# Delta rule stage of a 15-stage decoder: the formings of a unit move behind the groups of products, the projections between the couplings

## The chip, the cores and the metric

The kernel runs on one core of one Trainium2 chip. The metric is the device time of one execution in microseconds (us); lower is better. Three runs of the kernel before gave a median of 6915.6 us (6914.33 to 6922.18).

The engines are named as the profile names them: PE (TensorE, matrix multiplies into PSUM), DVE (VectorE), ACT (ScalarE), POOL (GpSimd). Each takes its instructions strictly in the program's order; they meet at semaphores.

## The reference

The whole reference is a decoder of four layers (attention, cross attention and feed forward in each), run over x of 16 sequences x 128 positions x 256 features. The change lies in its first step alone, a gated delta rule with 8 heads of size 64 and M = 8 modes. Cut to what matters:

```python
q = (x @ Wq).reshape(B, T, H, DK)
k = (x @ Wk).reshape(B, T, H, DK)
v = (x @ Wv).reshape(B, T, H, DV)
beta = sigmoid(x @ Wbeta); tg = sigmoid(x @ Wtg)          # one per head and mode
qr = l2norm(rotary(q, cos, sin)) * scale; kr = l2norm(rotary(k, cos, sin))
g = log(clip(tg * rho, 1e-06))
def step(S, inp):                                         # scanned over the T positions
    q_t, k_t, v_t, b_g, b_beta = inp
    S = S * exp(b_g)[..., None, None]
    kv = einsum('mbhk,mbhkv->mbhv', k_t, S)
    dv = (v_t[None] - kv) * b_beta[..., None]
    S = S + k_t[..., :, None] * dv[..., None, :]
    return S, einsum('mbhk,mbhkv->mbhv', q_t, S)
o = einsum('tmbhv,hm->bthv', ys, softmax(mode_logits))
x = layernorm(x + (o * sigmoid(x @ Wg)) @ Wo)
```

The kernel doesn't scan. For each of the head-mode pairs the recurrence over 128 positions is a triangular system, which is solved in blocks of 32 positions: the four 32x32 diagonal blocks are inverted, and the solution is built up quarter by quarter.

## The kernel before

`delta_stage` is the first of 15 stages. Its loop runs over the B = 16 sequences, one **turn** each (turn 0 and turn 15 are written out, 1 to 14 are a loop), and a turn has two **halves** of 4 heads. A half of a sequence is a **unit**: unit u = 2g is the first half of sequence g, u + 1 the second. A unit has 32 head-mode pairs, taken in GROUPS = 8 groups of four. The order on every engine is written out by hand, in a function `turn` for each engine (PE L886, ACT L1056, DVE L1300, POOL L698).

What a unit goes through, with the functions and lines:

- `phase` (PE L816), for each group i: three matmul steps put the decay exponents of four pairs into bank 0 (L824 to L828), ACT takes them through Exp (`decays`, L1017), four key and query products go to banks 4 and 5 (i even) or 1 and 2 (i odd) (L843), and DVE multiplies products and decays into NB (`take_products`, L1182). Exponents i + 1 wait for decays i, products i + 2 for the taking of products i. The rotated keys and queries that the products read are made by DVE (`rotate`, L1166) and POOL (`add_halves`, L691, two additions for each pair of groups, started when both of DVE's halves are there).
- `take_lower` (ACT L1024) copies the diagonal blocks out when the products are taken; `invert` (DVE L1203) inverts them in a chain of 61 small linked steps (L1219, L1224, L1225, L1227). Steps of the next sequence's projections (sums of squares L1241, decays, normalising L1248, splitting of the logarithms L1271 to L1279, and two parts of rounding L1283, L1289) are placed at given positions of that chain in the first half, two rotations at positions 40 and 46 in the second. DVE works in order: a placed step that has to wait holds up the inversion behind it.
- `spread` (ACT L1040) puts the inverse into the block diagonal Df; `form` (PE L798) multiplies Df with group i of the unit (8 matmul instructions of 128x256), and `take_formed` (ACT L1006) copies it back into NB (L1011, L1013). `set_identities` (ACT L1032) writes the diagonal blocks.
- `couple(u, half, q)` (PE L848), q = 1, 2, 3: for each of 4 heads one carrier matmul (L734) and 8 couplings, 16 matmul instructions of 64 columns (L860); `solutions` (ACT L1049) takes each head. `output` (PE L865) and `project_out` (L880) follow, and DVE adds and normalises.
- For the next sequence: `turn_x` (PE L736), `project_qk` (L743), `project_bt` (L751), `sum_logs` (L758), `turn_qk` (L769), `swap` (L777), `project_v` (L783), with `take_x`, `square` (L967), `sigmoids`, `logarithms`, `take`, `take_v` on ACT. `project_gates` (L790) and `take_gates` (L1000) serve the sequence at hand.

The order around the change, as PE has it in a turn. **First half**: the 8 groups of `phase` for unit u + 1, with forming 0 of unit u behind group 2 and forming 1 behind group 5, the earlier sequence's `project_out` behind group 4; then gates, form 2, turn_x, form 3, project_qk, form 4, project_bt, form 5 to 7, couple 1, sum_logs, turn_qk, couple 2, swap, couple 3, output. **Second half**: the 8 groups of `phase` for unit u + 2 (the next sequence), again with two formings (of unit u + 1) inside, then form 2 to 4, project_v, form 5 to 7, couple 1 to 3, output. ACT follows the same order. The formings use banks 6 and 7, and those of groups 3, 5 and 7 banks 4 and 5, so that one can run while ACT empties the other.

## Time and profile before

| | us |
|---|---|
| median of 3 runs | 6915.6 |
| the profiled execution | 6926.1 |
| its span on the core | 6924.3 |
| delta rule stage, in the span | about 95 to 2520 |
| one turn in the middle (first half, second half) | 74.86 + 75.46 = 150.3 |
| PE busy in this turn | 64.73 + 61.35 = 126.1 |
| DVE busy in this turn | 51.47 + 46.20 = 97.7 |

A span's views are in us from its start. In a timeline a line is one instruction or a run of like ones; the bracket is the idle time of the engine before it and what ended it. "issue" there means that the profile names no releaser.
### The profile page before, as it was taken

To read this page: it belongs to the slowest core of one execution; us is meant where nothing else is said; L and a number is where in the kernel's file an instruction comes from. 1 tells how busy PE (TensorE), PEld (TensorE's weight loads), DVE (VectorE), ACT (ScalarE), POOL (GpSimd) and SP (SyncE) were. 2 spreads that over 40 slices of the span, in tenths; PEclk is the share of its full clock that TensorE was granted. 3 is DMA by queue.
4 is the path that set the end of the run, shared out by engine and by line. 5 is a ranking of instruction groups with operands and counts; after the bars stand their busy time and mean duration, and the time that the engine had idled before them with its cause. 6 is when DMAs were issued, how large, how long until landed. Compare 5 with 4: busy or idle time off the path is not lost. (4 is left out here: it accounts for less than half of the span.)

```text
span 6924.3 us, 79364 instructions
## 1 busy us (share of the span) xinstructions
PE 5430.9 (78%) x28132; PEld 3808.8 (55%) x28132; DVE 3468.1 (50%) x7576; ACT 2177.9 (31%) x3691; POOL 1032.2 (15%) x845
## 2 busy tenths in 40 slices
PE   3888888888888875999998877547678467788698
PEld 1666666666666654566665555324356235565454
DVE  6666666666666633000004545558825445544445
ACT  2554544555454431212121222311123322232111
POOL 1212222222212212000002222000001002222000
PEclk8888888888888887999998878755578578888799
DMA  0000000000000000000000000000000000000000
GB/s 31 1 1 1 1 1 1 1 1 1 1 1 1 1 20 39 13 12 24 12 12 7 0 26 9 11 3 0 0 34 0 5 8 0 21 6 1 12 18 24
DMA packets 13489, 63.01 MB, mean 9 GB/s; under 512 B 1168, under 2 KB 5648, under 8 KB 11152
## 3 DMA queue, kind: packets, MB, share of 16 engines
q1 hardware_dynamic: 13200, 59.17, 2.4%
q8 instruction: 180, 2.95, 0.2%
q14 instruction: 109, 0.89, 0.0%
HBM read 57.07 MB, written 2.10 MB: 9 GB/s over the span
## 5 line engine op out<-in xcount | busy, mean ns | idle before, releaser
L1484 PE MATMUL psum<-arena 128*128 128x512 f32 x1600 | 706.6, 595 | 58.4 <-DVE Y L1548 35.8
L812 PE MATMUL psum<-arena 128*128 128x256 f32 x2048 | 559.8, 430 | 60.8 <-ACT arena L1013 59.6
L1565 DVE SCALAR_TENSOR_TENSOR Y<-psum,arena,Y 128x256 f32<-128x256 f32 x416 | 172.5, 477 | 847.9 <-PE psum L1496 847.9
L860 PE MATMUL psum<-arena 64*32 64x64 f32 (+2 forms) x6144 | 596.9, 272 | 0.0
L1496 PE MATMUL psum<-arena 128*128 128x256 f32 x2624 | 583.0, 380 | 4.1 <-DVE arena L1589 4.1
L1189 DVE TENSOR_TENSOR arena<-psum,arena 128x1024 f32<-128x1024 f32 x256 | 313.2, 1223 | 511.3 <-PE psum L843 331.4
L696 POOL TENSOR_TENSOR arena<-arena 128x512 f32<-128x512 f32 x256 | 327.1, 1298 | 1580.4 <-DVE arena L1179 1580.4
L1496 PEld LDWEIGHTS psum<-arena 128*128 128x128 f32 x2624 | 499.3, 190 | 111.8 <-issue 43.5
L1484 PEld LDWEIGHTS psum<-arena 128*128 128x128 f32 x1600 | 304.4, 191 | 409.1 <-issue 341.4
L812 PEld LDWEIGHTS psum<-arena 128*128 128x128 f32 x2048 | 429.4, 216 | 179.1 <-ACT arena L1013 74.5
L860 PEld LDWEIGHTS psum<-arena 64*32 64x32 f32 (+2 forms) x6144 | 517.5, 144 | 13.9 <-issue 7.8
L144 POOL TENSOR_TENSOR arena<-arena,eps 128x4 f32<-128x4 f32 (+2 forms) x76 | 15.0, 197 | 3234.9 <-DVE arena L139 3234.9
L843 PE MATMUL psum<-arena 64*128 64x256 f32 x2048 | 298.7, 411 | 129.2 <-POOL arena L696 129.2
L1530 ACT ACTIVATE arena<-psum,arena 128x512 f32<-128x512 f32 x256 | 175.9, 687 | 701.5 <-PE psum L1484 701.5
L422 PE MATMUL psum<-ident,arena 128*128 128x128 f32 x1280 | 218.0, 326 | 210.0 <-ACT arena L493 210.0
L402 PE MATMUL psum<-arena 128*128 128x512 f32 x640 | 356.8, 691 | 16.8 <-ACT arena L482 11.2
L1225 DVE TENSOR_TENSOR weights<-weights 128x30 f32<-128x30 f32 (+14 forms) x960 | 335.0, 349 | 33.5
L1224 DVE TENSOR_TENSOR weights<-weights 128x30 f32<-128x30 f32 (+14 forms) x960 | 331.0, 345 | 31.0
L1053 ACT ACTIVATE arena<-psum 32x512 f32<-32x512 f32 x384 | 226.2, 589 | 377.0 <-PE psum L860 376.4
L414 PEld LDWEIGHTS psum<-arena 128*128 128x128 f32 x2048 | 284.8, 217 | 101.6 <-issue 61.5
L422 PEld LDWEIGHTS psum<-ident,arena 128*128 128x128 f32 x1280 | 179.2, 171 | 232.2 <-ACT arena L493 232.0
L300 POOL TENSOR_TENSOR arena<-arena,weights 128x1024 f32<-128x1024 f32 x128 | 242.3, 1901 | 407.4 <-PE psum L402 341.7
(435 smaller groups left out, 8881.8 us busy)
## 6 DMA issues: line engine op xcount, KB each, us to landing
arena<-in_experts_L_ffn SPq DMA_DIRECT2D x8, 2052.0 KB, 8.3
arena<-in_ctxT SPq DMA_DIRECT2D x16, 512.0 KB, 3.3
arena<-in_experts_L_ffn SPq DMA_DIRECT2D x18, 384.0 KB, 3.0
weights<-in_w_L_attn SPq DMA_DIRECT2D x1, 3106.0 KB, 13.3
weights<-in_w_L_ffn SPq DMA_DIRECT2D x1, 3072.0 KB, 10.0
weights<-in_w_L_ffn SPq DMA_DIRECT2D x1, 2753.0 KB, 12.0
weights<-in_w_L_relu SPq DMA_DIRECT2D x1, 2436.0 KB, 8.9
X<-in_x SPq DMA_DIRECT2D x1, 2048.0 KB, 8.3
```

The costliest lines, as they stand in the source:

```text
L402: mm = nc.tensor.matmul(out[:, b * 4:b * 4 + 4, :], qT[:, c, u * P:(u + 1) * P], km[:, at % 2, b * 4:b * 4 + 4, :], start=True, stop=True)
L414: mm = nc.tensor.matmul(o_psum[:, c * HH + h, :], pT[:, j % 2, h, :], v, start=True, stop=True)
L422: mm = nc.tensor.transpose(pt_psum[:, h, :], pr[:, j % 2, h, :], k.ident[:, :])
L696: pool.tensor_tensor(both_, both_, t1[:, j, :, :], ALU.add).then_inc(s["rotated"], 1)
L812: mm = nc.tensor.matmul(ps[:, at + j // 2, (j % 2) * 2 * P:(j % 2 + 1) * 2 * P], Df[:, c, :], both(hf)[:, :, c, :], start=True, stop=True)
L843: mm = nc.tensor.matmul(ps[:, bank, m * 2 * P:(m + 1) * 2 * P], kq[rows, i // 2 % 2, at, 0, :], kq[rows, i // 2 % 2, at, :, :], start=True ...
L860: mm = nc.tensor.matmul(ps[n:n + Q, 4 + h, m * DK:(m + 1) * DK], NB[0:n + Q, 2 * (u_odd), place(h, m), n:n + Q], ur[0:n + Q, h, m, :], sta ...
L1189: dve.tensor_tensor(both(hf)[:, :, group, :].rearrange("p k c t -> p c k t"), products, bc(NB[:, 2 * hf + 1, group, :], 2, 2), ALU.mult).t ...
L1224: linked(dve.tensor_tensor(part, bc(inv[:, j + 1:, j], 2, j), bc(inv[:, j, 0:j], 1, below), ALU.mult))
L1225: linked(dve.tensor_tensor(inv[:, j + 1:, 0:j], inv[:, j + 1:, 0:j], part, ALU.add))
L1484: mm = nc.tensor.matmul(ps[:, bank, :], W[s][name][:, c, f * P:(f + 1) * P], xT[:, g, c, :], start=(c == 0), stop=(c == C - 1))
L1496: mm = nc.tensor.matmul(out, h[:, m % 2, f, u * P:(u + 1) * P], W[s]["w2"][:, f, :], start=(f == 0), stop=(f == FC - 1))
```

## The change

PE and ACT: in both halves forming i - 1 of the one unit now stands behind group i of `phase` of the other, for i = 1 to 7, so seven formings lie inside the phase and one (7) behind it. All but forming 7 use banks 6 and 7, and each of them waits for the one before to be copied; forming 7 uses banks 4 and 5. In the first half `turn_x` stands behind forming 7, then couple 1, `project_qk` and `project_bt`, couple 2, `sum_logs` and `turn_qk`, couple 3, `swap`, output. In the second half `project_v` stands in front of forming 7, and the couplings follow it. ACT takes in the same order; `set_identities` moves behind `logarithms` (first half) and behind the solutions of couple 1 (second half). DVE: five of the placed steps of the first half's inversion move by two positions (squares to 18, splitting to 36 and 38, first part to 50). Nothing is added to or taken from the work.

```diff
--- before.py
+++ after.py
@@ -800,13 +800,11 @@
                 if i == 0:
                     pe.wait_ge(s["inverse_ready"], u + 1)
                     need(pe, "solution_ready", u * (NQ - 1) * HALF)
-                elif i < 4:
+                elif i < 7:
                     pe.wait_ge(s["couplings_formed"], u * GROUPS + i)
-                else:
-                    pe.wait_ge(s["couplings_formed"], u * GROUPS + i - 1)
-                if i == 3 and products is not None:
+                elif products is not None:
                     pe.wait_ge(s["products_taken"], products)
-                at = 4 if i in (3, 5, 7) else 6
+                at = 4 if i == 7 else 6
                 for j in range(4):
                     c = 4 * i + j
                     mm = nc.tensor.matmul(ps[:, at + j // 2, (j % 2) * 2 * P:(j % 2 + 1) * 2 * P], Df[:, c, :],
@@ -887,41 +885,35 @@
                 u = g * HALVES
                 for i in range(GROUPS):
                     phase(g, u + 1, 1, i)
-                    if i in (2, 5):
-                        form(u, 0, i // 3)
+                    if i:
+                        form(u, 0, i - 1)
                     if i == 4 and (not isinstance(g, int) or g):
                         project_out(g - 1)
                 project_gates(g)
-                form(u, 0, 2)
+                form(u, 0, 7, (u + 1) * GROUPS + GROUPS - 1)
                 if more:
                     turn_x(g + 1)
-                form(u, 0, 3, (u + 1) * GROUPS + GROUPS - 1)
+                couple(u, 0, 1)
                 if more:
                     project_qk(g + 1)
-                form(u, 0, 4)
-                if more:
                     project_bt(g + 1)
-                for i in range(5, GROUPS):
-                    form(u, 0, i)
-                couple(u, 0, 1)
+                couple(u, 0, 2)
                 if more:
                     sum_logs(g + 1)
                     turn_qk(g + 1)
-                couple(u, 0, 2)
+                couple(u, 0, 3)
                 if more:
                     swap(g + 1)
-                couple(u, 0, 3)
                 output(u, g, 0, 0)
                 output(u, g, 0, 1)
                 for i in range(GROUPS):
                     if more:
                         phase(g + 1, u + 2, 0, i)
-                    if i in (2, 5):
-                        form(u + 1, 1, i // 3)
-                for i in range(2, GROUPS):
-                    form(u + 1, 1, i, (u + 2) * GROUPS + GROUPS - 1 if more and i == 3 else None)
-                    if more and i == 4:
-                        project_v(g + 1)
+                    if i:
+                        form(u + 1, 1, i - 1)
+                if more:
+                    project_v(g + 1)
+                form(u + 1, 1, 7, (u + 2) * GROUPS + GROUPS - 1 if more else None)
                 couple(u + 1, 1, 1)
                 couple(u + 1, 1, 2)
                 couple(u + 1, 1, 3)
@@ -1006,7 +998,7 @@
             def take_formed(u, hf, i):
 
                 act.wait_ge(s["formed"], u * GROUPS + i + 1)
-                at = 4 if i in (3, 5, 7) else 6
+                at = 4 if i == 7 else 6
                 formed = ps[:, at:at + 2, :].rearrange("p b (c k t) -> p (b c) k t", c=2, k=2)
                 nc.scalar.copy(NB[:, 2 * hf + 1, 4 * i:4 * i + 4, :], formed[:, :, 1, :])
                 for q in range(1, NQ):
@@ -1057,53 +1049,45 @@
                 u = g * HALVES
                 for i in range(GROUPS):
                     decays(u + 1, 1, i)
-                    if i in (2, 5):
-                        take_formed(u, 0, i // 3)
+                    if i:
+                        take_formed(u, 0, i - 1)
                     if i in (5, 6):
                         take_lower(u + 1, 1, 0, (2 * i - 10, 2 * i - 9))
                 take_lower(u + 1, 1, 1, range(NQ))
                 take_gates(g)
-                take_formed(u, 0, 2)
+                take_formed(u, 0, 7)
                 if more:
                     take_x(g + 1)
-                take_formed(u, 0, 3)
+                solutions(u, 1)
                 if more:
                     square(g + 1)
-                take_formed(u, 0, 4)
-                if more:
                     sigmoids(g + 1)
-                for i in range(5, GROUPS):
-                    take_formed(u, 0, i)
-                    if i == 5:
-                        set_identities(u + 1, 1)
+                solutions(u, 2)
                 if more:
                     logarithms(g + 1)
-                solutions(u, 1)
+                set_identities(u + 1, 1)
                 if more:
                     round_sums(g + 1)
                     take(g + 1, qkT, "qk_turned", "qkT_ready")
                     round_rest(g + 1)
-                solutions(u, 2)
+                solutions(u, 3)
                 if more:
                     take(g + 1, qkS, "swapped", "swapped_ready")
-                solutions(u, 3)
                 spread(u + 1)
                 for i in range(GROUPS):
                     if more:
                         decays(u + 2, 0, i)
-                    if i in (2, 5):
-                        take_formed(u + 1, 1, i // 3)
+                    if i:
+                        take_formed(u + 1, 1, i - 1)
                     if more and i in (5, 6):
                         take_lower(u + 2, 0, 0, (2 * i - 10, 2 * i - 9))
                 if more:
                     take_lower(u + 2, 0, 1, range(NQ))
-                for i in range(2, GROUPS):
-                    take_formed(u + 1, 1, i)
-                    if more and i == 4:
-                        take_v(g + 1)
-                    if more and i == 5:
-                        set_identities(u + 2, 0)
+                    take_v(g + 1)
+                take_formed(u + 1, 1, 7)
                 solutions(u + 1, 1)
+                if more:
+                    set_identities(u + 2, 0)
                 solutions(u + 1, 2)
                 solutions(u + 1, 3)
                 if more:
@@ -1312,11 +1296,11 @@
                     state["ch"].end()
                 steps = []
                 if more:
-                    steps += [(16, lambda: sum_squares(g + 1)), (22, lambda: scale_decays(g + 1)),
+                    steps += [(18, lambda: sum_squares(g + 1)), (22, lambda: scale_decays(g + 1)),
                               (24, lambda: clip_decays(g + 1)), (32, lambda: normalise(g + 1)),
-                              (38, remember("views", lambda: split(g + 1))),
-                              (40, lambda: split_rest(g + 1, state["views"])),
-                              (52, lambda: first_part(g + 1)), (58, lambda: second_part(g + 1))]
+                              (36, remember("views", lambda: split(g + 1))),
+                              (38, lambda: split_rest(g + 1, state["views"])),
+                              (50, lambda: first_part(g + 1)), (58, lambda: second_part(g + 1))]
                 if not first:
                     steps += [(2, remember("ch", lambda: finish(g - 1))), (14, applied)]
                 invert(u + 1, between(*steps))
```

## Rows read from the trace of the kernel before

**Rows 1.** The page: span of the profiled execution, and busy time of each engine.

```profile
span 6924.3 us, 79364 instructions
PE 5430.9 (78%) x28132; PEld 3808.8 (55%) x28132; DVE 3468.1 (50%) x7576; ACT 2177.9 (31%) x3691; POOL 1032.2 (15%) x845
```

**Rows 2.** Busy time in stretches: first half, second half of a turn, whole stage.

```profile
core 0: us, PE busy (x) PEld busy (x) DVE busy (x) ACT busy (x) POOL busy (x), PEclk, DMA share, GB/s
1201.93:1276.79 74.86, 64.73 (x507) 50.05 (x507) 51.47 (x107) 39.47 (x80) 18.95 (x17) 0.91 0.01 1
1276.79:1352.25 75.46, 61.35 (x450) 48.08 (x449) 46.20 (x88) 35.53 (x71) 14.06 (x12) 0.80 0.00 1
...
95.00:2520.00 2425.00, 2009.98 (x15220) 1564.82 (x15220) 1553.57 (x3103) 1192.50 (x2386) 522.35 (x462) 0.85 0.01 2
```

**Rows 3.** Timeline of PE, first half: start us, length us, instructions [idle before <-releaser].

```profile
1201.93 0.38 PE L824 MATMUL psum<-arena 128*128 128x512 bf16 x1 [2.73 <-issue]
...
1208.91 1.13 PE L843 MATMUL psum<-arena 64*128 64x256 f32 x8 [2.51 <-POOL arena L696]
1209.97 1.99 PE L812 MATMUL psum<-arena 128*128 128x256 f32 x8
1211.80 0.38 PE L824 MATMUL psum<-arena 128*128 128x512 bf16 x1
...
1232.78 0.41 PE L740 MATMUL psum<-ident,weights 128*128 128x128 f32 x2 [2.16 <-ACT arena L1003]
...
1236.41 4.33 PE L748 MATMUL psum<-weights 128*128 128x512 f32 x8
...
1251.04 0.16 PE L734 MATMUL psum<-arena 128*128 128x1 bf16 x1 [2.95 <-issue]
```

**Rows 4.** Timeline of PE: second half, and the last turn of the stage.

```profile
1307.14 6.58 PE L812 MATMUL psum<-arena 128*128 128x256 f32 x16 [3.12 <-ACT arena L1013]
...
1323.56 0.16 PE L734 MATMUL psum<-arena 128*128 128x1 bf16 x1 [2.94 <-issue]
...
2476.99 1.99 PE L812 MATMUL psum<-arena 128*128 128x256 f32 x8 [1.14 <-ACT arena L1013]
...
2493.35 0.16 PE L734 MATMUL psum<-arena 128*128 128x1 bf16 x1 [1.19 <-issue]
```

**Rows 5.** Timeline of DVE over the same turn.

```profile
1203.86 1.23 DVE L1189 TENSOR_TENSOR arena<-psum,arena 128x1024 f32<-128x1024 f32 x1 [14.35 <-PE psum L843]
...
1230.76 1.91 DVE L1219 STREAM_TRANSPOSE weights<-weights 128x1024 f32<-128x1024 f32 x1 [2.65 <-ACT weights L1029]
...
1241.41 1.22 DVE L1241 TENSOR_REDUCE arena<-arena 128x16 f32<-128x1024 f32 x1 [2.37 <-ACT arena L970]
...
1254.46 0.22 DVE L1279 TENSOR_TENSOR weights<-arena,weights 128x64 f32<-128x64 f32 x1
...
1269.49 0.69 DVE L1174 TENSOR_TENSOR arena<-arena,weights 128x512 f32<-128x512 f32 x1 [1.88 <-ACT arena L984]
...
1280.08 1.23 DVE L1189 TENSOR_TENSOR arena<-psum,arena 128x1024 f32<-128x1024 f32 x1 [4.58 <-ACT arena L1021]
...
1306.04 1.92 DVE L1219 STREAM_TRANSPOSE weights<-weights 128x1024 f32<-128x1024 f32 x1 [2.65 <-ACT weights L1029]
...
1334.07 2.07 DVE L1227 STREAM_TRANSPOSE weights<-weights 128x1024 f32<-128x1024 f32 x1
```

**Rows 6.** Timeline of ACT over the same turn.

```profile
1228.14 2.58 ACT L1029 ACTIVATE weights<-arena 32x512 f32<-32x512 f32 x4 [1.36 <-DVE arena L1189]
...
1278.09 1.28 ACT L1021 ACT_TABLE_LOAD   x1
...
1346.30 4.20 ACT L1046 COPY arena<-weights 32x1024 f32<-32x1024 f32 x4
```

**Rows 7.** Busy time in stretches in which PE runs couplings alone.

```profile
1323.60:1343.60 20.00, 20.00 (x175) 18.13 (x176) 13.18 (x27) 5.66 (x10) 2.60 (x2) 0.50 0.01 2
2493.40:2506.70 13.30, 13.30 (x204) 12.08 (x204) 0.00 (x0) 6.48 (x11) 0.00 (x0) 1.00 0.01 1
```

## The prediction

> **What bounds the kernel now.** I read the page first for the size of the stage, then the stretches of one turn in the middle, then the timelines of PE, DVE and ACT over that turn, to see which wait ends last at each place. The stage takes 2425 us of the span of 6924.3 [rows 1, 2]. A turn takes 74.86 + 75.46 = 150.3 us; PE is busy for 64.73 + 61.35 = 126.1 of it and DVE for 97.7 [rows 2]. So no engine is full, but PE is the nearest to it, and the reader should see two losses of PE.
>
> The first is idle time, 10.1 us in the first half and 14.1 in the second. It has few places: 2.5 us before the third group of products, which waits for POOL's rotation; 2.2 before turn_x, whose bank ACT frees with the gates; 2.95 before the first coupling of either half, where ACT is two copies behind; 3.1 before the forming at 1307.14, which waits for the copy of the last [rows 3, 4]; and 2.7 at the loop's end.
>
> The second loss is the clock. Behind the 2.94 us of idling at 1323.56 PE runs the couplings at a granted clock of 0.50 for 20 us: 175 instructions, at 17 to a head 10.3 heads, so 1.94 us a head. In the last turn the wait at the same place is 1.19 us, the clock stays at 1.00, and 204 instructions (12 heads) take 13.3 us, 1.11 a head [rows 4, 7]. Twelve heads cost 23.3 us or 13.3.
>
> DVE isn't the bound yet: it waits 14.35 us for the first products of the first half, and 4.58 for ACT's decays in the second [rows 5]. It will matter what is left of these 19 us.
>
> **The change, part by part.** Nothing is added; all gains and losses are waits and clock. I walk through one new turn from a = 0, the start of the first taking of products in the first half (1203.86 in the old turn [rows 5]). Three steps repeat: exponents and products of a group, 1.83 us (1209.97 less 1.13 and the exponents before it, and the same as eight groups without waits give); a forming, 1.83 us (1209.97 to 1211.80) [rows 3]; a forming with the copy behind it on ACT, 3.13 us (1.99 and the 1.14 waited [rows 4]).
>
> *First half, phase.* A group and a forming together are 3.66 us. The rotation chain runs from the taking of products 0 (1203.86) to products 2 (1208.91), 5.05 us [rows 3, 5]. PE now has one more forming in it, so the wait of 2.5 falls to 0.7, and the later ones vanish (a pair of groups now takes 7.3 us). The copy of a forming has 3.66 us before the next one needs the bank and takes 3.13, so the single pair of banks costs nothing; if the copy took over 0.5 us longer, every step would. The last group ends at 26.2, forming 6 at 28.0, gates at 29.9, forming 7 at 31.7. ACT copies forming 6 until 29.3 and only then takes the lower blocks (2.58 us [rows 6]): DVE's inversion starts at 31.9. It started at 1230.76 - 1203.86 = 26.9 [rows 5], so it loses 5.0.
>
> *Between phase and couplings.* ACT then loads its table and takes the gates (1.9 us), and turn_x starts at 33.9 after 2.1 us of idling, as before (2.16). The copy of forming 7 ends at 34.8, and couple 1 starts at 34.9 instead of 1251.04 - 1203.86 = 47.2 [rows 3, 5]. But project_qk (4.3 us [rows 3]) and project_bt (half as many matmuls of a quarter of the columns, 0.5) have gone behind it.
>
> *Couple 1 and the squares.* In the old turn idling of 2.2 and 0.4 us at this place was followed by a lower clock at project_qk (eight matmuls in 4.33 us; at the high clock some 3.5). Now 2.1 and 0.5 stand right before couplings, which haven't brought the clock back by themselves for 20 us [rows 7]. If it falls: couple 1 7.4 us, project_qk 5.6 (its first half still low). If not: 4.5 and 3.5. Bounds for the pair are 8.0 and 14.8 (all low). The sum of squares on DVE starts 0.7 behind project_qk (1236.41 + 4.33 to 1241.41 [rows 3, 5]): at 48.7, or 43.7. DVE's chain arrives there at 41.0 (31.9, and 9.1 us for the 18 links; 16 took 8.3), so it waits **7.7 or 2.7 us** where it waited 2.37. This is the new wait of the change; behind it stands the whole inversion.
>
> *The logarithms.* From the start of the sum of squares to the end of splitting were 1254.46 + 0.22 - 1241.41 = 13.2 us with 24 links between [rows 5]; now 20 links, 1.7 less: 11.5. sum_logs on PE can start at 60.2, or 55.2. PE is ready (bt 0.6, couple 2 4.5) at 53 or 48, so it idles for **7 us**, and the clock falls; sum_logs and turn_qk take some 4.5, couple 3 4.5 to 5, swap 1.8 (as many columns as a forming), ACT's copy 0.7. The swapped keys are there at 72.0 or 67.0. DVE has ended its inversion by then (70 or 65), so its rotation follows at once. From there to the first taking of the second half it is two rotations (four steps of 0.6, 2.4), POOL's pair (2.6, which is the 5.05 from above less a taking and half a rotation) and the products (1.1), with half a microsecond for DVE and POOL in each other's way 6.6 us; ACT's spread and table load (4.20 + 1.28 + 0.6 [rows 6]) fit under it. So the second half's first taking is at **78.6 or 73.6**, against 1280.08 - 1203.86 = 76.2: the first half loses 2.4 or gains 2.6.
>
> *Second half*, from b = 0 at that taking. The same walk without project_out: inversion starts at 30.0 (before: 1306.04 - 1280.08 = 26.0 [rows 5]). project_v and forming 7 are done at 29.8, couple 1 starts at 31.6 after 1.8 us of idling, nearer to the 1.19 that left the clock up than to 2.94. Couplings end at 45, or 55 if it falls; with output 3.7 (what the 26 us from the first coupling to the loop's end leave beside 12 heads) and the loop's 2.7, PE is back at 51 or 61. DVE inverts in 1334.07 + 2.07 - 1306.04 = 30.1 us [rows 5], so the inverse is there at 60.1; ACT spreads it by 64.3 (4.20 [rows 6]), and the next decays follow, 64.9, first taking 65.0. **DVE and ACT are the bound here**, at either clock of PE. The one cost that I can't see is ACT's own turn of the loop, which was hidden. DVE's is below 1.0 and PE's 2.7 [rows 3]; 0 and 2.7 are the ends, and I take 1.0, since ACT's instructions are few and long like DVE's. So 66.0, against 150.3 - 76.2 = 74.1: a gain of 8.1.
>
> *set_identities*, 3.15 us on ACT, now stands between solutions of couplings 1 and 2 in the second half; PE has 4.5 us of couple 2 above it, and it is free. If it weren't, it would cost up to 3 us of PE that isn't the bound. In the first half it stands under the 7 us of idling.
>
> **The sum.** A new turn takes 78.6 + 66.0 = 144.6 us when the clock falls before couple 1, and 139.6 when it doesn't. The same idling fell on a lower clock in each old turn, but it is now split by turn_x a little differently; I take two turns in three low: 143.0, a gain of 7.3. Fifteen turns give 110. The last turn gains about 7 in its first half and loses 4 in its second, where seven formings stand alone at 3.13 us with one pair of banks. The first turns have less to gain; I take 10 off. Against the profiled execution of 6926.1 that is 6823; that execution is 10 us over the median of the runs, so the forecast is **6815 us**.
>
> A rule of the Trainium skill stands against one step. Rows 7 show couplings alone for 20 us at 0.50 with PE busy throughout. "TensorE: Matmul & The Clock Gate", section "Part 1: The HAM clock gate", has it that sustained activity releases the throttle. By that rule couple 1 would win its clock back before it ends; the trace disagrees. It is the first rival below.
>
> **Rivals.**
> 1. *The clock stays up or comes back during couple 1.* Then every turn takes 139.6: 15 x 10.7 less the 10, about 6765. For it: 1.19 us of idling was harmless, and PE's other waits shrink. Against: rows 7, and 2.6 us idle of 3.2 just before. Chance 0.13.
> 2. *ACT pays PE's price at the loop and the clock is low in each turn*: 146.3, gain 4.0, 15 x 4.0 less the 7 is 6863. Chance 0.09.
> 3. *Slower: the low clock holds through the whole first half.* Couple 1 at 7.8 leads into project_qk all low (7.0), couple 2 doesn't raise it, and after 7 us of idling sum_logs, turn_qk, couple 3 (7.8) and swap (3.5) are low as well. Squares at 50.5, split at 62, swapped keys at 79, taking at 85.6: the first half loses 9.4 and the second gains 8.1 less what ACT's loop costs beyond 1.0. That is +1.3 to +3.0 a turn, 6935 to 6960. It decides when low stretches add up to over 30 us of the half; the old half had 10 around couple 1, and full-width matmuls ended them. Chance 0.12.
> 4. *No change*: each step of the phase is 0.5 us longer than its matmuls, because ACT now has decays and copy in each (1.7 of 3.66 us, and 1.3 more of lower blocks in two of them). That is 7 us over both phases, the whole gain; 6915. ACT has the room by the rows, so 0.06.
>
> **How the numbers follow.** The forecast has 0.60: 6815, with its own range 6790 to 6840. The range wanted holds rivals 1 and 2 and most of the forecast's errors: 6755 to 6880; outside remain rivals 3 and 4 (0.18). Faster by over 0.2% (14 us, about what a measurement of this kernel can tell): 0.60 + 0.13 + 0.09 = 0.82; same 0.06; slower 0.12.
>
> **What would show it.** In the changed turn: forming and group in steps of 3.66 with one wait of about 0.7; couple 1 35 us behind the first taking; a wait of DVE before L1241 of 3 to 8 us; PE idle for some 7 before L763; second half 66 us from first taking to first taking, with PE waiting for ACT's decays (L1021) right after the loop. The forecast is wrong if PE's couplings of the second half still end last, if L763 doesn't wait, or if steps in the phase are longer than 3.66.

## The result: faster by 0.6%, a third of what was forecast

Over eleven executions of each, the changed kernel has a median of 6882.1 us (6837.0 to 6888.1) and the kernel before 6914.3 us (6904.4 to 6922.2). The ratio is 0.9942, with a 95% interval of 0.9924 to 0.9961. The forecast was 6815, with a range of 6755 to 6880. The direction was right; the gain is 32 us where 100 were forecast, and the time lies just above the range.

| | before | forecast | changed |
|---|---|---|---|
| median, us | 6914.3 | 6815 | 6882.1 |
| profiled execution, us | 6926.1 | | 6883.7 |
| a turn in the middle | 150.3 | 143.0 (139.6 or 144.6) | 146.75 |
| first half, taking to taking | 76.2 | 73.6 or 78.6 | 81.24 |
| second half, taking to taking | 74.1 | 66.0 | 65.51 |

The changed kernel's executions fall in two groups, two of the eleven at 6837 to 6838 with a mean granted clock of 0.825 and nine at 6880 to 6888 with 0.815 or 0.816; in a run shown further down a turn of the shorter kind is profiled.

These are the stretches of the changed kernel's turn, cut at the first taking of products of each half (columns as in [rows 2]):

```profile
span 6881.9 us, 79230 instructions
...
1180.11:1261.35 81.24, 68.91 (x504) 52.24 (x508) 50.32 (x108) 41.77 (x82) 18.99 (x17) 0.84 0.00 1
1261.35:1326.86 65.51, 56.79 (x446) 44.79 (x449) 45.89 (x89) 32.52 (x68) 14.11 (x12) 0.81 0.01 2
```

PE is still busy for 126 us of the turn, but the granted clock, PEclk, is lower than before in the first half (0.84, it was 0.91 [rows 2]). The second half has become 8.6 us shorter, the first 5.0 us longer. The timeline of DVE shows where (it answers to [rows 5]; L1203 is the start of an inversion, L1225 the sum of squares, L1173 the taking of products):

```profile
1213.63 1.92 DVE L1203 STREAM_TRANSPOSE weights<-weights 128x1024 f32<-128x1024 f32 x1 [3.03 <-ACT weights L1021]
...
1231.33 1.22 DVE L1225 TENSOR_REDUCE arena<-arena 128x16 f32<-128x1024 f32 x1 [8.62 <-ACT arena L962]
...
1254.18 0.69 DVE L1158 TENSOR_TENSOR arena<-arena,weights 128x512 f32<-128x512 f32 x1 [0.59 <-ACT arena L976]
...
1261.35 1.23 DVE L1173 TENSOR_TENSOR arena<-psum,arena 128x1024 f32<-128x1024 f32 x1 [1.18 <-PE psum L841]
...
1291.81 1.92 DVE L1203 STREAM_TRANSPOSE weights<-weights 128x1024 f32<-128x1024 f32 x1 [3.03 <-ACT weights L1021]
...
1326.86 1.23 DVE L1173 TENSOR_TENSOR arena<-psum,arena 128x1024 f32<-128x1024 f32 x1 [2.71 <-ACT arena L1013]
```

The new wait is the 8.62 us before L1225: DVE stands in the middle of the inversion and waits for the squares, which wait for project_qk, which now stands behind couple 1. The old one was 2.37. On PE the same turn reads (answers to [rows 3, 4]):

```profile
1215.66 0.41 PE L740 MATMUL psum<-ident,weights 128*128 128x128 f32 x2 [2.24 <-ACT arena L995]
1216.55 0.16 PE L734 MATMUL psum<-arena 128*128 128x1 bf16 x1 [0.48 <-issue]
...
1224.36 6.29 PE L748 MATMUL psum<-weights 128*128 128x512 f32 x8
...
1243.00 0.80 PE L763 MATMUL psum<-weights 128*128 128x128 f32 x2 [7.53 <-DVE weights L1263]
...
1293.43 0.16 PE L734 MATMUL psum<-arena 128*128 128x1 bf16 x1 [1.91 <-issue]
...
1320.83 0.38 PE L823 MATMUL psum<-arena,weights 128*128 128x512 bf16 x1 [2.98 <-issue]
...
1326.81 0.61 PE L822 MATMUL psum<-arena 128*128 128x512 bf16 x1 [3.73 <-ACT arena L1013]
```

Waits of 2.24 and 0.48 us stand before couple 1, 7.53 before sum_logs, 1.91 before couple 1 of the second half, and at the turn's end 2.98 and 3.73. Couple 1 and the greater part of project_qk run at the low clock, and so do heads two to ten of the second half's couplings and the start of the next phase:

```profile
1216.60:1230.50 13.90, 13.90 (x77) 9.58 (x78) 5.47 (x20) 3.06 (x6) 0.75 (x2) 0.53 0.00 1
1294.60:1310.30 15.70, 15.70 (x138) 14.22 (x137) 14.43 (x40) 7.72 (x11) 0.00 (x0) 0.50 0.01 2
1326.80:1332.00 5.20, 5.19 (x18) 3.34 (x19) 4.10 (x6) 0.60 (x1) 2.49 (x2) 0.50 0.00 0
```

### The profile page after: what moved, and what is told of

It reads as the page before. It is cut to its first block and busy times, and to the rows that moved or that the text cites. A ratio compares the mean times of both kernels' runs of the same rounds, so it can differ in the third digit from the quotient of the medians.

```text
span 6881.9 us, 79230 instructions
## 1 busy us (share of the span) xinstructions
PE 5420.1 (79%) x28029; PEld 3790.1 (55%) x28132; DVE 3447.2 (50%) x7576; ACT 2165.4 (31%) x3691; POOL 1033.8 (15%) x845
## 5 line engine op out<-in xcount | busy, mean ns | idle before, releaser
L1480 PE MATMUL psum<-arena 128*128 128x256 f32 x2624 | 583.0, 380 | 4.1 <-DVE arena L1573 4.1
L1480 PEld LDWEIGHTS psum<-arena 128*128 128x128 f32 x2624 | 499.3, 190 | 111.7 <-issue 43.5
L1173 DVE TENSOR_TENSOR arena<-psum,arena 128x1024 f32<-128x1024 f32 x256 | 313.5, 1224 | 458.7 <-ACT arena L1013 237.6
L1468 PEld LDWEIGHTS psum<-arena 128*128 128x128 f32 x1600 | 304.4, 191 | 409.1 <-issue 341.4
L810 PE MATMUL psum<-arena 128*128 128x256 f32 x2048 | 520.4, 398 | 9.8 <-ACT arena L1005 6.9
L810 PEld LDWEIGHTS psum<-arena 128*128 128x128 f32 x2048 | 379.3, 195 | 139.9 <-issue 84.2
L841 PE MATMUL psum<-arena 64*128 64x256 f32 x2048 | 329.3, 445 | 57.9 <-POOL arena L696 57.9
L1209 DVE TENSOR_TENSOR weights<-weights 128x30 f32<-128x30 f32 (+14 forms) x960 | 335.0, 349 | 33.5
L414 PEld LDWEIGHTS psum<-arena 128*128 128x128 f32 x2048 | 284.8, 217 | 101.7 <-issue 61.6
```

The source lines that it names most:

```text
L414: mm = nc.tensor.matmul(o_psum[:, c * HH + h, :], pT[:, j % 2, h, :], v, start=True, stop=True)
L810: mm = nc.tensor.matmul(ps[:, at + j // 2, (j % 2) * 2 * P:(j % 2 + 1) * 2 * P], Df[:, c, :], both(hf)[:, :, c, :], start=True, stop=True)
L841: mm = nc.tensor.matmul(ps[:, bank, m * 2 * P:(m + 1) * 2 * P], kq[rows, i // 2 % 2, at, 0, :], kq[rows, i // 2 % 2, at, :, :], start=True ...
L1173: dve.tensor_tensor(both(hf)[:, :, group, :].rearrange("p k c t -> p c k t"), products, bc(NB[:, 2 * hf + 1, group, :], 2, 2), ALU.mult).t ...
L1209: linked(dve.tensor_tensor(inv[:, j + 1:, 0:j], inv[:, j + 1:, 0:j], part, ALU.add))
L1468: mm = nc.tensor.matmul(ps[:, bank, :], W[s][name][:, c, f * P:(f + 1) * P], xT[:, g, c, :], start=(c == 0), stop=(c == C - 1))
```

## The experiments

The theory after the result: the changed kernel's **first half is bound by a chain through the next sequence's projections** (couple 1, project_qk, squares, splitting, sum_logs, couple 3, swap), its length set partly by PE's clock in couple 1 and project_qk; the **second half by DVE's inversion and ACT's spread**. I shall call it theory A. The rivals: the new order of projections helps and the loss is elsewhere; DVE's inversion is the bound everywhere and its wait was free; PE's low clock in the second half is what a turn pays. In each group of runs the kernel before ran on the same chip: 6919.2 for the first four, 6916.4 for the next four, 6905.0 for the last two. Differences in us to the changed kernel take its median of 6882; an execution of its shorter group (6837) is 45 us below that.

### The two parts apart

**Only the moved formings** (the changed kernel with the old order behind the first half's phase; PE's part, ACT's order and DVE's positions follow it):

```diff
                 if more:
                     turn_x(g + 1)
-                couple(u, 0, 1)
-                if more:
                     project_qk(g + 1)
                     project_bt(g + 1)
-                couple(u, 0, 2)
+                couple(u, 0, 1)
                 if more:
                     sum_logs(g + 1)
                     turn_qk(g + 1)
-                couple(u, 0, 3)
+                couple(u, 0, 2)
                 if more:
                     swap(g + 1)
+                couple(u, 0, 3)
```

> The changed kernel with the first half's old order behind the phase: project_qk and project_bt ahead of couple 1, sum_logs and turn_qk behind couple 1, swap behind couple 2, DVE's steps at their old positions; only the moved formings of the change are left. Theory A (the first half of the changed kernel is bound by the chain couple 1, project_qk, squares, splitting of the logarithms, sum_logs, and couple 1 standing ahead of project_qk lengthens it): DVE waits under 1 us before L1225 instead of 8.6, a turn is 138 to 141 us instead of 146.8, time about 6760 to 6800. Rival B (the projections between the couplings help, as they fill PE's waits): slower than the changed kernel, over 6882. Rival C (a turn is bound by DVE's inversions wherever PE's steps stand): no change, 6875 to 6890.

Measured: 6831.9 us, ratio 0.9872 (0.9855 to 0.9888); a turn is 143.4 us. Rival B falls, and rival C by its range; but the changed kernel's own shorter group, which the sections below come to, is as fast as this run (6837, 143.4 a turn). DVE's wait before the squares is 0.7 us, as theory A had it, but the turn missed A's 138 to 141 and the time its 6760 to 6800 by 32 us. The reason is on PE:

```profile
1160.80:1239.06 78.26, 64.51 (x504) 49.27 (x508) 50.39 (x107) 41.77 (x82) 18.94 (x17) 0.88 0.00 1
1239.06:1304.19 65.13, 55.17 (x446) 43.93 (x450) 46.50 (x89) 32.52 (x68) 14.12 (x12) 0.86 0.01 2
...
1216.99 0.80 PE L763 MATMUL psum<-weights 128*128 128x128 f32 x2 [9.19 <-DVE weights L1261]
```

In the old order sum_logs stands behind couple 1 alone, and with the formings gone from this place nothing is left in front of it: PE waits 9.19 us for the splitting, and then has couples 2 and 3 still to do before output. So the change's order has a good step (sum_logs behind couple 2) and a bad one (project_qk behind couple 1). The run with project_qk first, further down, has the good step without the bad one and is 74 us faster than this.

**Only the couplings' new order**, with the formings where they were (PE's part again):

```diff
                 form(u, 0, 3, (u + 1) * GROUPS + GROUPS - 1)
-                if more:
-                    project_qk(g + 1)
-                form(u, 0, 4)
-                if more:
-                    project_bt(g + 1)
-                for i in range(5, GROUPS):
+                for i in range(4, GROUPS):
                     form(u, 0, i)
                 couple(u, 0, 1)
                 if more:
+                    project_qk(g + 1)
+                    project_bt(g + 1)
+                couple(u, 0, 2)
+                if more:
                     sum_logs(g + 1)
                     turn_qk(g + 1)
-                couple(u, 0, 2)
+                couple(u, 0, 3)
                 if more:
                     swap(g + 1)
-                couple(u, 0, 3)
```

> The kernel before with the other part of the change alone: the formings stay where they were (two inside the phase, six behind it), but couple 1 stands ahead of project_qk and project_bt, couple 2 ahead of sum_logs, couple 3 ahead of swap, DVE's steps at their new positions. Theory A: the squares come some 8 us later than in the kernel before, sum_logs waits for the splitting, a turn gets 5 to 10 us longer than before, time 6985 to 7060. Rival B (this part helps by itself): under 6905.

Measured: 6983.6 us, ratio 1.0092 (1.0075 to 1.0108), 1 us under theory A's 6985 to 7060; its 5 to 10 us a turn are 4.1 on average over the loop (153.9 where the kernel before has 149.8). Rival B falls. By itself this part makes the kernel slower. DVE waits in the inversion for

```profile
1290.46 1.22 DVE L1235 TENSOR_REDUCE arena<-arena 128x16 f32<-128x1024 f32 x1 [19.07 <-ACT arena L968]
```

19 us, and the first half takes 86.0 us in this turn, where it took 76.2. In most other turns of this run the wait is 17.5 us and the half 83.5.

### One step undone, one wait filled

**project_qk ahead of couple 1**, all else as changed:

```diff
                 if more:
                     turn_x(g + 1)
-                couple(u, 0, 1)
-                if more:
                     project_qk(g + 1)
                     project_bt(g + 1)
+                couple(u, 0, 1)
                 couple(u, 0, 2)
```

with `square` and `sigmoids` ahead of the first solutions on ACT, `logarithms` ahead of the second. This brings back the old place of the step, and with it what the clock does there.

> The changed kernel with one thing undone: project_qk and project_bt stand ahead of couple 1 again (with their ACT steps ahead of the solutions, and logarithms ahead of the second solutions). Everything else as changed. Theory A: DVE's wait before L1225 falls from 8.6 to under 1 us, the wait of PE before L763 from 7.5 to under 4, the second half starts 6 to 9 us earlier in the turn, which is 138 to 141 us; time 6755 to 6800. Rival C (DVE's inversion is the bound in the first half too, and its wait was free): 6875 to 6890. Rival D (only the clock before couple 1 counts): couple 1 at the high clock, and no more than 4 us a turn, 6820 to 6850.

Measured: 6757.8 us, ratio 0.9764 (0.9748 to 0.9781), in theory A's range; C and D fall. The placing of this one step, its clock included, costs 6882 - 6758 = 124 us (79 against the shorter group), more than the 87 us (6919 - 6832) that the moved formings gain in the old order. The lines that answer to those above:

```profile
1124.19:1196.16 71.97, 62.37 (x504) 48.10 (x508) 50.30 (x107) 41.86 (x82) 19.02 (x17) 0.93 0.00 1
1196.16:1262.09 65.93, 56.63 (x446) 44.70 (x449) 45.60 (x89) 32.52 (x68) 14.11 (x12) 0.84 0.01 2
...
1166.03 1.21 DVE L1224 TENSOR_REDUCE arena<-arena 128x16 f32<-128x1024 f32 x1
...
1177.71 0.79 PE L763 MATMUL psum<-weights 128*128 128x128 f32 x2 [4.57 <-DVE weights L1262]
```

DVE no longer waits for the squares, PE waits 4.57 instead of 7.53 us before sum_logs (a little over the "under 4" expected), the first half is 9.3 us shorter and the second is the same but for 0.4. The turns of the loop alternate between 137.9 and 138.6 us. Couple 1 runs at the high clock here (1.08 us for a head's 16 couplings, 1.91 in the changed kernel); what the clock alone is worth is for the next run to tell.

**Idle matmuls before couple 1 of the first half**, to keep the clock up:

```diff
+            def warm(n, taken=None):
+                if taken is not None:
+                    pe.wait_ge(s["products_taken"], taken)
+                for _ in range(n):
+                    nc.tensor.matmul(ps[:, 1, 0:D], ident_h, later_h[:, 0:2, :], start=True, stop=True)
...
                 form(u, 0, 7, (u + 1) * GROUPS + GROUPS - 1)
+                warm(18, (u + 2) * GROUPS)
                 if more:
                     turn_x(g + 1)
+                warm(5)
                 couple(u, 0, 1)
```

> The changed kernel with idle matmuls (18 bf16 ones of 256 columns into the free bank 1 before turn_x, 5 behind it) where PE waits 2.2 and 0.5 us ahead of couple 1 in the first half. No work is left out. Theory A with the clock as the forecast had it: the clock stays at 1.00 through couple 1 and project_qk, which take 4.5 and 3.5 us instead of 7.8 and 6.1, the squares come some 5 us earlier, and a turn is 140 to 142 us instead of 146.8; 6790 to 6820. Rival C (DVE-bound): no change. Rival E (couplings by themselves bring the clock down, filled wait or not): granted clock 0.50 in couple 1 as before, no change.

Measured: 6806.8 us, ratio 0.9837 (0.9821 to 0.9854), in theory A's range. Couple 1 runs at the full clock and the wait before the squares falls to 2.60:

```profile
1139.44:1215.36 75.92, 66.02 (x527) 51.35 (x531) 50.44 (x107) 41.97 (x82) 19.00 (x17) 0.90 0.00 1
1215.36:1280.48 65.12, 54.25 (x446) 42.82 (x449) 46.48 (x88) 32.52 (x68) 14.12 (x12) 0.85 0.01 2
1175.80:1180.40 4.60, 4.60 (x70) 4.17 (x70) 4.14 (x16) 1.97 (x5) 0.75 (x2) 1.00 0.00 0
...
1184.61 1.22 DVE L1234 TENSOR_REDUCE arena<-arena 128x16 f32<-128x1024 f32 x1 [2.60 <-ACT arena L971]
```

The wait before sum_logs is 7.53 us as before, and the turns are 140.2 to 141.1 us. So the low clock in couple 1 and project_qk costs 75 us of the 124 in this place, and the order by itself the other 49. Against the shorter group the same two runs give 30 and 49. That the clock only costs because project_qk stands behind couple 1 is argued from the chain; no run has the low clock in couple 1 with project_qk ahead of it.

### The second half

**Idle matmuls before couple 1 of the second half alone** (`warm(18, (u + 3) * GROUPS)` ahead of `couple(u + 1, 1, 1)`):

> The changed kernel with 18 idle matmuls into bank 1 ahead of couple 1 in the second half alone, where PE waits 1.9 us and then runs ten heads of couplings at the low clock. No work is left out. Theory A (the second half is bound by DVE's inversion and ACT's spread, 65.1 to 65.9 us in every kernel so far, with the couplings done 9 to 14 us before): couplings at the high clock, PE ready some 8 us earlier, and no gain: a turn 146 to 147 us, time 6870 to 6890. Rival F (PE's low clock there is what a turn pays): 8 us a turn, about 6765.

Measured: 6837.0 us, ratio 0.9886 (0.9869 to 0.9902). Neither expectation on the time held. On the mechanism theory A did:

```profile
1160.84:1239.14 78.30, 66.22 (x507) 50.69 (x508) 50.40 (x108) 41.98 (x82) 19.02 (x17) 0.87 0.00 1
1239.14:1304.21 65.07, 51.73 (x467) 39.79 (x466) 46.43 (x89) 32.32 (x68) 14.10 (x12) 0.90 0.01 2
1271.00:1284.30 13.30, 13.30 (x205) 12.00 (x205) 12.02 (x37) 9.29 (x14) 0.00 (x0) 1.00 0.02 3
```

The couplings of the second half now run at 1.00 and end 45.2 us behind the first taking instead of 52.9, and the half is 65.07 instead of 65.51: 7.7 us of PE's time gave 0.4 at most. Rival F falls. But the first half, which was not touched, is 78.30 instead of 81.24. Couple 1 there loses the clock later than it did and takes 6.1 us instead of 7.8, and the squares come 3.5 us earlier. This first half is the one of the changed kernel's own shorter group, shown in the next run (78.24), and so is the time (6837). The filler didn't make a new pattern; all four executions with it are of the shorter one, where 7 of 23 without it are (two of eleven, and three and two of six in the next two runs). That suggests that what PE does in one half bears on where the low stretches fall in the other.

**Ten tiny memsets in the second half's inversion**, meant as a delay of 1 us:

```diff
-                    invert(u + 2, between((40, lambda: rotate(g + 1, u + 3, 1, 0, 0)),
+                    idle = [(at, lambda n=at - 22: dve.memset(logs[:, 12 * n:12 * n + 12], 0.0)) for at in range(22, 32)]
+                    invert(u + 2, between(*idle, (40, lambda: rotate(g + 1, u + 3, 1, 0, 0)),
```

> The changed kernel with ten tiny memsets (12 columns each) placed between links of the second half's inversion, about 1 us of DVE in all. If a turn is a plain chain through that inversion: the second half 66 to 66.8 us, a turn 147.5 to 148, 8 to 15 us slower, 6890 to 6900. If the turn's length is held by where its low stretches of PE's clock fall (as the second group of executions and the fillers in the second half suggest): a turn unchanged to 0.1 us, or 3 us off to either side, with the first half making up the difference: 6880 to 6885 or about 6837 or 6930.

As a delay it failed: each memset takes 0.07 us between two links and the inversion lasts 30.1 us as before. It is in effect the changed kernel again (median 6859.0, ratio 0.994, 0.9911 to 0.997), and its six executions show both groups: three at 6831 to 6837, three at 6881. The profiled one is of the shorter group:

```profile
1163.70:1241.94 78.24, 66.17 (x507) 50.59 (x508) 50.33 (x108) 41.97 (x82) 19.01 (x17) 0.87 0.00 1
1241.94:1307.07 65.13, 54.33 (x449) 42.63 (x448) 46.62 (x99) 32.52 (x68) 14.10 (x12) 0.85 0.01 2
...
1211.34 1.22 DVE L1225 TENSOR_REDUCE arena<-arena 128x16 f32<-128x1024 f32 x1 [5.73 <-ACT arena L962]
```

A turn is 143.37 us; DVE's wait before the squares is 5.73 instead of 8.62, and the second half is 65.13 instead of 65.51. **The changed kernel once more:**

> The changed kernel itself once more, for its profile: 6880 to 6884 with turns of 146.8 us, or (two of eleven executions so far) 6837 with turns that I expect at 143.4 us, in which the first half has a shorter low stretch around couple 1 and the second half is the same 65.1 to 65.5.

Measured: median 6880.3; four executions at 6880 to 6885, two at 6830 and 6837; ratio 0.9941 (0.9914 to 0.9968). Its profile is of the longer group and repeats the first one: 81.27 and 65.47 us. So the two groups differ by 3.4 us a turn, 3.0 of it in the first half, where the squares come 3.6 us earlier. In either group every turn of the middle repeats the last one to 0.1 us, low stretches included. What sends an execution into the one or the other stays open. The same turn of 143.37 us, to 0.02 us, stands in three kernels whose waits differ: in this one, in the one with the moved formings alone and in the one with the second half's wait filled. So a turn isn't the plain sum of its steps, and differences of up to 3.4 us a turn (some 50 us) between two of these kernels may come from the pattern and not from the edit. What sets it stays open too.

### What is left, and a better balance

**project_qk early and fillers in three places** (18 before turn_x, 18 before couple 1 of the second half, and 16 behind the first group of products of the first half):

> The kernel with project_qk and project_bt ahead of couple 1 (run before at 6758), with idle matmuls before turn_x (18), before couple 1 of the second half (18) and behind the first group of products of the first half (16). Theory A (both halves are now bound by DVE's inversions and what hangs on them, PE's clock hardly counts): 0 to 2 us a turn, 6725 to 6758. Rival F (PE's clock is the bound): over 4 us a turn, under 6700.

Measured: 6754.4 us, ratio 0.9767 (0.9750 to 0.9783), as theory A had it: 3 us less than the 6757.8 without the fillers on another chip, and by the ratios (0.9767 and 0.9764) nothing. With project_qk early, filling the waits before the couplings is worth nothing.

**The same fillers in the changed kernel** (and 5 behind turn_x):

> The changed kernel with idle matmuls in all three places (18 and 5 around turn_x, 18 before couple 1 of the second half, 16 behind the first group of products of the first half). Theory A (beyond couple 1, the clock low at the start of the phase costs the first half what the forecast missed): the inversion of the first half starts 31.9 to 32.3 us behind the first taking instead of 33.5, a turn is 138.5 to 140.5 us against about 141 with the first two fillers alone, 6770 to 6800. If the low clock at the phase's start costs nothing: equal to the run with the fillers around turn_x alone, 6800 to 6812.

Measured: 6802.4 us, ratio 0.9835 (0.9818 to 0.9851), 4 us under the run with the first two fillers, and by the ratios (0.9835 and 0.9837) equal to it. From the second turn on the turns are 140.2 to 141.2 us, as there, not 138.5 to 140.5. The inversion starts between 32.8 and 34.0 us behind the first taking, without the steady gain expected. The third filler didn't do what it was meant for, and PE's timeline shows why (L741 is the filler):

```profile
1274.34 3.60 PE L741 MATMUL psum<-arena 128*128 128x256 bf16 x16
1282.49 0.61 PE L829 MATMUL psum<-arena 128*128 128x512 bf16 x1 [4.56 <-ACT arena L1026]
...
1282.50:1287.50 5.00, 5.00 (x18) 3.16 (x19) 3.92 (x6) 0.60 (x1) 2.46 (x2) 0.50 0.02 3
```

Its products had been taken long before, so it runs at once and 4.56 us of idling are left behind it; the next 5 us of the phase are at 0.50 as they were. It is the same in the run before (4.57). So neither run says what the low clock at the phase's start costs. By the profile alone, the first group's products and the first forming take 2.08 and 2.86 us in the changed kernel, where later ones take 1.13 and 1.99: 1.8 us together.

**Three formings inside the phase instead of seven**, on top of project_qk early:

```diff
                     phase(g, u + 1, 1, i)
-                    if i:
-                        form(u, 0, i - 1)
+                    if i in (1, 3, 5):
+                        form(u, 0, i // 2)
...
                 project_gates(g)
-                form(u, 0, 7, (u + 1) * GROUPS + GROUPS - 1)
+                form(u, 0, 3, (u + 1) * GROUPS + GROUPS - 1)
+                form(u, 0, 4)
                 if more:
                     turn_x(g + 1)
+                form(u, 0, 5)
+                if more:
                     project_qk(g + 1)
+                form(u, 0, 6)
+                if more:
                     project_bt(g + 1)
+                form(u, 0, 7)
```

with the banks in turn as in the kernel before, and the same in the second half. Three things change at once against the run with project_qk first: the number of formings in the phase, the banks, and the projections between the formings.

> The same order with project_qk early, but only three formings inside each phase (behind groups 1, 3 and 5) and five behind it, with the two pairs of banks in turn as in the kernel before, project_v between formings 4 and 5 in the second half. Theory A (a forming inside the phase puts off the products and so the inversion of the other unit by 1.83 us, and the inversions are now the bound): inversions start 26 to 28 us behind the first taking instead of 33 and 25 to 26 instead of 30; the second half takes 60 to 61 us from taking to taking instead of 65.1; a turn 128 to 134 us, time 6600 to 6700. Rival G (the formings back behind the phase bring back the idling and the low clock of the kernel before, PE becomes the bound): a turn 139 us or more, 6760 to 6850.

Measured: **6663.4 us**, ratio 0.9631 (0.9613 to 0.9649): faster than both kernels, by 253 and by about 220 us; rival G's times fall. Timeline of DVE (L1218 starts an inversion, L1226 ends it), and the stretches:

```profile
1113.94 1.96 DVE L1218 STREAM_TRANSPOSE weights<-weights 128x1024 f32<-128x1024 f32 x1 [2.65 <-ACT weights L1029]
...
1122.99 1.21 DVE L1240 TENSOR_REDUCE arena<-arena 128x16 f32<-128x1024 f32 x1
...
1180.01 1.98 DVE L1218 STREAM_TRANSPOSE weights<-weights 128x1024 f32<-128x1024 f32 x1 [2.65 <-ACT weights L1029]
...
1086.59:1154.48 67.89, 60.15 (x507) 45.53 (x507) 52.43 (x107) 41.47 (x82) 19.46 (x17) 0.98 0.00 1
1154.48:1217.22 62.74, 56.12 (x449) 43.59 (x449) 47.49 (x88) 32.64 (x68) 14.54 (x12) 0.85 0.01 2
...
992.42 0.16 PE L734 MATMUL psum<-arena 128*128 128x1 bf16 x1 [1.19 <-issue]
...
996.21 1.91 PE L860 MATMUL psum<-arena 64*32 64x64 f32 x16
...
1010.41 0.75 DVE L1282 SCALAR_TENSOR_TENSOR arena<-arena,weights,psum 128x512 f32<-128x512 bf16 x1 [3.79 <-ACT arena L989]
...
1127.32 0.16 PE L734 MATMUL psum<-arena 128*128 128x1 bf16 x1 [1.19 <-issue]
...
1127.41 1.08 PE L860 MATMUL psum<-arena 64*32 64x64 f32 x16
```

The inversions start 27.3 and 25.5 us behind the first taking instead of 33.5 and 30.5, the squares don't hold DVE up, PE's wait before sum_logs is gone, and a turn is 129 to 136 us. This spread goes with PE's clock. In seven of the fifteen first halves it stays at 1.00 through couple 1 (the turn at 1127), and the half takes 67.0 to 67.9 us; in the other eight it falls (the turn at 992), and the half takes 72.3 to 73.8, with DVE waiting up to 3.8 us for the rounding on ACT behind sum_logs. So by the profile PE's clock counts again in this kernel's first half; no run fills the wait here. The second half came to 61.1 to 62.7 where 60 to 61 was expected: at its end PE is last again by a little, as ACT has spread the inverse and waits 0.77 us for PE's exponents, and the products behind them take 2.08 us at the low clock.

## Why the prediction was wrong

The step that failed is the sum of the first half. The forecast took 78.6 us in two turns of three and 73.6 in the third; it measured 81.24 in every turn of the loop. The waits in it were the right ones; their sizes and how often the clock falls were not.

**The second half: right.** Forecast 66.0 us, measured 65.51 (65.07 to 65.96 in the profiled turn of every kernel with seven formings in the phase). The inversion starts at 30.5 (30.0 forecast), and lasts 30.1; ACT's spread ends at 1326.13, and its decays begin at 1326.16. So ACT's own turn of the loop, for which the forecast took 1.0 out of 0 to 2.7, costs nothing; this and the later start nearly cancel, which is luck of half a microsecond. That PE's clock has no say here was forecast and is shown by the filled wait that freed 7.7 us of PE and gave 0.4 at most. Only the clock itself was judged wrongly: 1.91 us of idling did lower it. The forecast leaned on one place where 1.19 us had left it up [rows 4]; in the changed kernel's own last turn 1.19 us at this place were followed by a low clock.

**The waits of the first half: right.** The walk had DVE's new wait (2.7 or 7.7; 8.62), PE's 7 us before sum_logs (7.53), the stall of 0.7 in the phase (0.69 in the run with the second half's wait filled) and the 3.66 us steps (3.64).

**The sizes in the first half: too small.** Forecast 73.6 or 78.6, measured 81.24. Three terms:
- *How often the clock falls before couple 1.* "Two turns in three" was a guess; it falls in each of the profiled turns. At 5 us for the third turn this is 1.7 us a turn. The filled wait measures the whole step at 81.24 - 75.92 = 5.3 us, against 5.0 in the walk.
- *The phase*. The inversion starts at 33.5 instead of 31.9 and couple 1 at 36.4 instead of 34.9; the second is what the chain pays. The forecast let PE wait at the loop for ACT's decays (2.98 and 3.73 us) and didn't ask what that does to the clock. The next 5 us of the phase run at 0.50, which by the profile makes 1.8 us. No run fills this wait, so that a full clock there would give them back isn't shown.
- *Couple 1 with project_qk*: 14.1 us (36.4 to 50.5) instead of 13.0.

The first one and the excess of 2.6 us over the low case, less 0.5 from the second half, make the 3.8 us between 143.0 and 146.8. From the first taking of turn 0's first half to that of turn 15 the two traces take 2243.9 and 2197.1 us: a gain of 46.8 where the forecast had 110 less 10, so 53 us of the 67 by which it was off. Nine more lie behind that, where the changed kernel's trace is 6.1 us longer and the forecast had 3 less; 7.5 of them are the last couplings, which took 13.3 us at the high clock [rows 7] and now take 20.8. Six are no kernel time at all: the forecast came from 6823 to 6815 because the profiled execution before was slow for its kernel, and the profiled one of the changed kernel is only 1.6 us over its median. Some 2 us gained ahead of turn 0's first half go the other way.

**The rivals.** The first (clock kept up) gave 139.6 a turn; with the fillers it is 140.2 to 141.2, so it was priced well, but didn't come by itself. The second (146.3 a turn) is nearest, and half by luck: the clock is low in each turn as it says, but ACT pays nothing at the loop. The third (slower) has the squares nearly right (50.5, measured 51.2), but couple 2 and couple 3 run at the high clock. The fourth (no change) didn't happen.

**What the walk failed to ask.** It priced project_qk behind couple 1 as one wait among others, and put the whole change down as one thing. The cause of the small gain, shown by undoing it alone, is this step: 124 us with its clock, 49 without. The forecast had all rows for it: the second half showed DVE and ACT to be the next bound, and then nothing that feeds DVE's chain may stand behind PE work that doesn't. And the formings in the phase have a price of their own: with four fewer of them the other unit's inversion starts on average 5.7 and 4.7 us earlier than with project_qk first, 1.2 to 1.4 us for each. Once DVE was named as the bound, that they put it off by 5.0 and 4.0 us in the walk itself should have been read as a loss to be balanced. With both mended the kernel runs in 6663 us; how much of the last 94 us is the formings' number, and how much the banks and the spread projections, wasn't separated.

## What to carry to other kernels

When two engines hand work back and forth, order the instructions of the one with slack by what the other waits for: here a projection of 4 us placed behind 4 to 8 us of couplings cost more than the whole gain of filling the waits. Work moved into a loop delays everything that follows the loop by what it doesn't spend in waits (here five formings more, 9.2 us, put the inversions off by 6.6 and 4.5); move in only as much as there are waits. And before a freed wait is booked as gain, look at what PE does at the new waits: the clock that it comes out of them with is part of their price.

## What the runs showed of the hardware

PE's clock seems to link parts of the kernel that share no data. With 18 idle matmuls before the couplings of the second half, these ran at 1.00 and the half gained 0.4 us at most, while all four executions were of the shorter group, whose first half is 2.9 us shorter. One program settled into two different, each exactly repeating patterns of low stretches, with turns of 146.8 or 143.4 us.

And one length of idling isn't a safe guide. 1.19 us before the last couplings left the clock at 1.00 in the kernel before [rows 4, 7], and at the same place of the changed kernel they were followed, 2 us later, by 14.3 us at 0.50. In the kernel with three formings in the phase PE idles 1.19 us before couple 1 in every half, and the clock fell in 21 of 32 and stayed up in 11.

"TensorE: Matmul & The Clock Gate" of the Trainium skill, section "Part 1: The HAM clock gate", says that sustained activity releases the throttle. In the changed kernel's turn the clock rose while PE ran project_qk (6.29 us). It didn't rise in 15.7 us of unbroken couplings, so there the trace disagrees; it came back 1 us later, still among couplings, in the tenth head (its 16 took 1.64 us, the next 1.08).
